# An attention and mixture-of-experts kernel: the first expert matrices are kept on the chip, and GpSimd's opening list has another order

## What is computed

```python
x = x + xattn(layernorm(x), ctx, mask, mask, Wq, Wkv, Wc)   # softmax(q k^T / sqrt(8)) v, then Wc
xf = layernorm(x).reshape(-1, 128)
top_vals, top_idx = top_k(xf @ router_w.T, 2)
probs = softmax(top_vals)
for e in range(8):
    w = sum(where(top_idx == e, probs, 0))
    h = gelu(xf @ w1[e].T + b1[e])         # 128 -> 512
    out = out + w * (h @ w2[e].T + b2[e])  # 512 -> 128
x = x + out
```

## Time and profile before

| | |
|---|---|
| median of three runs | 394.74 us |
| the profiled execution's own time | 396.63 us |
| its span, first to last instruction | 394.9 us |
| PE busy | 325.1 us (82%) |
| DVE, ACT, POOL busy | 253.1, 231.7, 231.8 us |
| chain that ended last, by engine | PE 65%, DVE 13%, issue 9%, ACT 6%, DMA 3%, POOL 1% |
| read from HBM | 34.90 MB |
| moved by DMA | 59.94 MB |

### The profile page before, as it was taken

One profiled execution on the slowest core, in us unless ns is written; L12 is line 12 of the kernel. 1 busy time (PEld: TensorE's weight loads), 2 busy tenths in 40 slices (PEclk: granted clock), 3 DMA queues, 4 the chain that ended last, 5 costly groups with the idle time before them and its releaser, 6 DMA issues.

```text
span 394.9 us, 11551 instructions
## 1 busy us (share of the span) xinstructions
PE 325.1 (82%) x3721; PEld 260.3 (66%) x3721; DVE 253.1 (64%) x751; ACT 231.7 (59%) x567; POOL 231.8 (59%) x384
## 2 busy tenths in 40 slices
PE   2659699999979898978787976969899999999950
PEld 1226466666656665656555865968789999999840
DVE  4855779999868778769943623645554555446762
ACT  2313569798868768667766423545456666566530
POOL 8745252724758567563667487565766656565550
PEclk9999989999999899999996888999999999999995
DMA  4664463555535424411143563666547767659946
GB/s 131 179 176 114 111 187 96 99 129 161 146 100 142 123 76 120 126 46 45 32 118 99 171 188 108 180 204 185 170 123 254 216 207 213 179 184 317 295 137 186
DMA packets 60618, 59.94 MB, mean 152 GB/s; under 512 B 13797, under 2 KB 45188, under 8 KB 60560
## 3 DMA queue, kind: packets, MB, share of 16 engines
q1 hardware_dynamic: 53504, 46.61, 42.6%
q0 software_dynamic: 4320, 8.47, 6.2%
q10 hardware_dynamic: 2736, 4.13, 3.3%
HBM read 34.90 MB, written 11.63 MB: 118 GB/s over the span
## 4 chain that ended last, share of the span: by engine, by line
PE 65%; DVE 13%; issue 9%; ACT 6%; DMA 3%; POOL 1%; another core or an unknown queue 1%; SPq 0%; DVEq 0%; POOLq 0%; ACTq 0%
PE sexp L1196 16%; PE smax L1184 16%; PE smax L1062 7%; PE tail L1106 7%; DVE shift L1351 4%; PE feed L1053 2%; PE feed L1038 2%; ACT probs L871 2%; PE prep L1130 2%; PE sexp L1070 2%; PE heads L1122 2%; PE feed L1048 2%; PE prep L1137 1%; DMA stacks<-result_d 1%
## 5 line engine op out<-in xcount | busy, mean ns | idle before, releaser
L1351 DVE TENSOR_REDUCE shift<-smax 128x4 f32<-128x512 f32 x128 | 87.0, 682 | 35.1 <-PE smax L1062 34.0
L1184 PE MATMUL smax<-probs,w_ring 128*128 128x128 f32 x568 | 79.2, 284 | 14.3 <-issue 12.8
L793 POOL DMA_INDIRECT result_d<-y_out,stacks x71 | 70.8, 997 | 30.5 <-issue 28.8
L1184 PEld LDWEIGHTS smax<-probs,w_ring 128*128 128x128 f32 x568 | 71.2, 197 | 17.7 <-issue 17.2
L871 ACT ACTIVATE probs<-sexp 128x512 f32<-128x512 f32 x128 | 74.4, 595 | 12.9 <-PE sexp L1070 11.6
L704 POOL DMA_INDIRECT dispatch_d<-rows_out,row_i x64 | 63.0, 984 | 30.6 <-issue 14.8
L1196 PE MATMUL sexp<-w_sb,probs 128*128 x568 | 78.6, 282 | 2.0 <-ACT probs L1005 1.2
L1826 DVE TENSOR_TENSOR probs<-smax,b_cols 128x512 f32<-128x512 f32 x71 | 49.0, 691 | 44.3 <-issue 15.9
L1196 PEld LDWEIGHTS sexp<-w_sb,probs 128*128 128x128 f32 x568 | 70.5, 195 | 5.8 <-issue 5.6
L1005 ACT ACTIVATE probs<-probs 128x512 f32<-128x512 f32 x71 | 44.8, 631 | 37.3 <-DVE probs L1826 27.3
L1062 PE MATMUL smax<-stacks 64*128 64x128 bf16 x512 | 51.3, 230 | 17.2 <-DVE shift L1351 9.7
(11 more groups left out here) (221 smaller groups left out, 502.6 us busy)
## 6 DMA issues: line engine op xcount, KB each, us to landing
w_ring<-w_t_dram SPq DMA_DIRECT2D x71, 256.0 KB
stacks<-kpart SPq DMA_DIRECT2D x46, 128.0 KB
stacks<-qpart SPq DMA_DIRECT2D x46, 128.0 KB
stacks<-dispatch_d SPq DMA_DIRECT2D x71, 65.0 KB
stacks<-result_d ACTq DMA_DIRECT2D x12, 256.0 KB
xw<-x_dram SPq DMA_DIRECT2D x8, 256.0 KB, 3.3
w_sb<-w_t_dram SPq DMA_DIRECT2D x8, 256.0 KB
out_dram<-xw SPq DMA_DIRECT2D x8, 256.0 KB
```

The costliest lines, as they stand in the source:

```text
L793: nc.gpsimd.indirect_dma_start(out=result_d, out_offset=bass.IndirectOffsetOnAxis(ap=xg[r][:, D + 1:D + 2].bitcast(U32), axis=0), in_=y_ou ...
L1184: last = nc.tensor.matmul(up_ps[i][:, c * P:(c + 1) * P], w1_ring[t % WRING][:, c * P:(c + 1) * P], xg_t[i], start=True, stop=True)
L1351: nc.vector.tensor_reduce(shift4[n % 2][:, hp, 0, 4 * m:4 * m + 4], smax[hp][:], AX.X, ALU.max, negate=True).then_inc(max_taken, 1)
```

## The change

A tile `w1_sb` of 128 partitions holds all eight w1 (16 KB a partition). SP loads one of them in each of the slots 2, 6, ..., 30, behind what else it does in the slot (`w1_here` counts them), and waits for all eight ahead of the first ring load. `load_w1` then copies the expert's part from `w1_sb` into the ring; ring, semaphores and order stay. In POOL's opening list `clear_queries(1)` and `set_keys(1)` change places around `split_low(0)`, `prepare_values(0)` goes ahead of the second row scales, and the third part of group 1's queries goes behind slot 0's `split_shift`.

```diff
--- before.py
+++ after.py
@@ -154,6 +154,7 @@
 
         router_sb = sb("router_sb", [P, EXPERTS])
         w1_ring = [sb(f"w1_ring{i}", [P, FF]) for i in range(WRING)]
+        w1_sb = sb("w1_sb", [P, EXPERTS, FF])
         w2_sb = sb("w2_sb", [P, EXPERTS, FC, D])
         b1_cols = sb("b1_cols", [P, EXPERTS * FC])
         b2_sb = sb("b2_sb", [P, EXPERTS * D])
@@ -327,6 +328,7 @@
         w2_loaded = sem("w2_loaded")
         xg_loaded = [sem(f"xg_loaded{i}") for i in range(TRING)]
         w1_loaded = [sem(f"w1_loaded{i}") for i in range(WRING)]
+        w1_here = sem("w1_here")
         xg_turned = sem("xg_turned")
         xg_copied = sem("xg_copied")
         up_done = sem("up_done")
@@ -493,6 +495,9 @@
                 if g is not None and g >= RING:
                     sp.wait_ge(v_done, g - RING + 1)
                     load_ctx(g)
+                if s % GB == 2:
+                    e = s // GB
+                    sp.dma_start(w1_sb[:, e:e + 1], w1_t[:, e:e + 1]).then_inc(w1_here, 16)
                 if s and s % GB == 0:
                     e = s // GB - 1
                     sp.dma_start(w2_sb[:, e:e + 1], w2_t[:, e:e + 1]).then_inc(w2_loaded, 16)
@@ -513,7 +518,7 @@
 
                 if t >= WRING:
                     sp.wait_ge(up_done, t - WRING + 1)
-                sp.dma_start(w1_ring[r][:], w1_t.rearrange("p e f -> p (e f)")[:, bass.ds(e * FF, FF)]).then_inc(w1_loaded[r], 16)
+                sp.dma_start(w1_ring[r][:], w1_sb[:].rearrange("p e f -> p (e f)")[:, bass.ds(e * FF, FF)]).then_inc(w1_loaded[r], 16)
 
             def store_pad(at):
                 sp.dma_start(dispatch_d[bass.ds(at, P), :], pad_row[:]).then_inc(pads_sent, 16)
@@ -521,6 +526,7 @@
             sp.wait_ge(table_steps, FIRST_STEPS)
             experts = table_values(mybir.EngineType.SP, expert_of, 0, EXPERTS - 1)
             starts = table_values(mybir.EngineType.SP, start_of, 0, EXPERTS * REGION)
+            sp.wait_ge(w1_here, 16 * EXPERTS)
             for t in range(AHEAD):
                 load_w1(t, t, experts[t])
             sp.wait_ge(sexp_done, UNITS * OLD_BATCHES)
@@ -635,15 +641,14 @@
             set_keys(0)
             clear_queries(0)
             query_scale(0)
+            clear_queries(1)
+            split_low(0, krest, kpart, k_split)
             set_keys(1)
-            split_low(0, krest, kpart, k_split)
-            clear_queries(1)
+            prepare_values(0)
             query_scale(1)
             scale_rows(1)
-            prepare_values(0)
             split_low(1, krest, kpart, k_split)
             query_scale(2)
-            split_low(1, qrest, qpart, q_split)
 
             def constants():
                 nc.gpsimd.iota(iota_i[:], [[1, EXPERTS]], base=EXPERTS, channel_multiplier=0).then_inc(iotas_made, 1)
@@ -724,6 +729,7 @@
                 if 0 < s <= BATCH:
                     split_shift(s - 1)
                 if s == 1:
+                    split_low(1, qrest, qpart, q_split)
                     set_keys(2)
                 if s == 2:
                     clear_queries(2)
```

## The result

The changed kernel took 401.85 us (median of 4 runs, 401.43 to 403.97) beside 394.93 us for the kernel before on the same chip (4 runs): a ratio of 1.0139, 95% interval 1.0091 to 1.0187. It is slower by 1.4%, and outside the range of the prediction. The profiled execution has a span of 399.8 us (before 394.9).

The account below looks back on a forecast made before the run. PE was taken to bound attention and the expert tiles, with engines waiting for each other in the opening. -0.75 and -2.1 us, with 0 for loads and loop, gave -2.85: 394.74 to 391.9 us, range 387.5 to 396.

Parts of the forecast that it names:

- The opening: GpSimd's reordered list up to the first scores: xq's gain is given back, qpart gains; -0.75 us, between 0.4 and -1.65.
- the turn: Behind the first scores, PE no longer waits for POOL's shift, so next scores start earlier; -2.1 us, bounds -1.5 and -2.44.
- slot 4's first maximum: Sign in attention of the profile after: slot 4 comes some 2.9 us earlier.
- The sum of -2.85 us for the order: GpSimd's new list: -0.75 us up to the first scores and -2.1 us behind them.
- Rival C: Opening: PE's speed rise stays where it is in time, half the gain comes back; -1.4 us, 393.3 us; chance 0.23.
- The eight loads and SP's wait at 0: Attention: eight 256 KB w1 loads on SP's queue and the wait for them cost 0, loads from 0 to +1 us.
- the loop stays PE's: 0: Expert tiles: copies from SBUF fit under PE's 1.91 us a tile, so the loop changes by 0.
- 1.16 + 0.48 us a tile: Tile loop's DMA engines: 1.16 us for the 256 KB copy, 0.48 for all else; 1.64 us, under 1.91.
- Rival D: Tile loop: copies out of SBUF become its bound; at 165 GB/s +9.6 us, 401.5 us in all; chance 0.13.
- Its second form: Tile loop: copies slow PE's own reads; 2.1% on 71 x 1.91 us would eat the whole gain; within the 0.13 chance.

Follow-up runs that it names:

- ring from DRAM: The changed kernel, with the eight resident loads and the wait, but the ring filled from DRAM as before; 0.9920 of before on chip B, 0.9965 on D.
- ring only: Against the kernel before: ring filled from the resident copy in SBUF, GpSimd's opening list in its old order; 1.0176 of before on chip B, 1.0226 on D.
- e9: Against the kernel without copies: whole copies from register-held SBUF addresses run beside PE, nothing reads or waits for them; 1.0088 of before on chip B.
- e4: The changed kernel without ring copies: PE reads the resident copy at a fixed expert, the expert's choice is left out; 0.9920 of before on chip B.

## Why the prediction was wrong

- **The opening: right, step by step.** Xq 0.69 us (0.69 said), moment_sum ended at 15.19 (15.2), qpart 0.70 (0.69), first scores at 20.31 (20.3), the turn at 26.28 (26.3), slot 4's first maximum 2.7 us earlier (2.9). The port held as the rows of before had shown it: what the COPY gave to xq it took from diff_sq. One detail differs: of the two small operations behind mean_diff only diff_sq stopped for the COPY; the ADD before it started with the COPY, at 11.50, and took 0.15 us.
- **The sum of -2.85 us for the order: right in size.** Alone the order gave -0.78% on B (3.1 us, 1.3 to 5.0) and -0.48% on D (1.9 us, 0.6 to 3.2). Rival C, in which the rise of PE's speed stays where it is in time and takes half of the gain back, falls: PE's score matmuls go from 0.31 to 0.22 us each at 39.93 us, before at 42.62, and attention stays some 3 us ahead.
- **The eight loads and SP's wait at 0: right** (0.9920 with, 0.9922 without).
- **The step that failed is "the loop stays PE's: 0".** It put the copies at nothing because their own time on the DMA engines, 1.16 + 0.48 us a tile, is under 1.91. That condition held, with room to spare: no DMA is among PE's waits, and in the changed kernel the engines' share is no higher than before:

```profile
300.00:340.00 40.00, 39.95 (x354) 39.56 (x353) 20.60 (x42) 26.23 (x62) 24.08 (x41) 1.00 0.61 200
```

  By that share a copy took some 0.7 us (an estimate, 0.61 x 1.91 - 0.48), not 1.16. What the sum has no term for is what a copy out of SBUF costs work that doesn't wait for it. Measured, that is 6.6 us on chip D, by the kernels that differ in the source of the ring alone. By the means of the stages, whole copies from a register-held place against none or DRAM, it is 3.7 us in tiles 2 to 30, 1.0 in tiles 30 to 63 (a tile costs 0.03 us more) and 1.0 in tiles 63 to 70, together 5.7. Only the last of these has a shown path, PE's register load at tile 64, which the prediction doesn't name. For tiles 2 to 30 the cause stays open: PE's idle time there (15.8 to 17.6 us in three profiles, 12.9 to 16.8 in six) and its time at half clock (some 9 to 18 and 7 to 11 us, estimated from the mean granted clock) overlap between the two sorts of kernel.
- **Rival D had the sign, with 0.13, and not the mechanism; that its 401.5 us lies beside the measured 401.85 is chance.** Copies too slow for the loop would have shown in PE's waits and as a longer tile throughout. Its second form, copies that slow PE's own reads, falls as well: on chip D the median of a first-product matmul is 275 ns in both kernels (ring from DRAM, then changed):

```profile
L1190 PE MATMUL smax<-probs,w_ring x568: 275/275/553, 213.6 to 376.9; 128*128 128x128 f32 x190
```

```profile
L1190 PE MATMUL smax<-probs,w_ring x568: 275/275/561, 213.2 to 381.3; 128*128 128x128 f32 x190
```

  The rule that the prediction cited from the Trainium skill, page "SBUF — State Buffer", section "SBUF: two separate sides", that a transfer doesn't slow an engine's access, agrees with these rows. The slowed accesses that the rows show are the sequencers' register loads. The Trainium skill's page "Runtime: NRT & Kernel Launch", section "Instruction fetch mechanics", says of register loads from HBM that each is a round trip over AXI. If those from SBUF go the same way, they belong to the transfers; the loads of 1.9 us (changed) and 2.8 us (ring only, both on chip D) fit that, and no run here shows the path itself.

What stays open: by what path the copies cost 3 to 4 us in tiles 2 to 30, why a register-held place in SBUF costs more than a fixed one (or the order in which the places are read does), how GpSimd's sends and PE's gaps hang together, and why chip C showed so little of the loss.

## What to carry to other kernels

A transfer that no one waits for isn't free (e9 lost 1.7% against e4), so look, besides bandwidth, at what the sequencers do beside it, register loads above all. A gap that is longer in one profile of after than in one of before may be there without the change as well: look for it in the kernel with half of the change. Moving a source nearer to save DRAM traffic is worth nothing where a DRAM ring already costs as much as no ring, and that one comparison, ring from DRAM against no copies, can be made first. Where runs spread and chips differ, set each half of a change beside the whole on one chip before a loss is explained.

## What the runs showed of the hardware

- Issuing a 256 KB copy of 128 rows took SP 333 ns from DRAM with a register-held address, 471 ns from SBUF at a fixed place, 492 ns from SBUF at a register-held one; the DRAM load issued behind it took 452 in place of 333 ns.
- A register load of up to eight values took PE 0.60 to 0.74 us at the median; the one at tile 64 took 1.07 to 1.08 us with the ring from DRAM or small copies, 1.5 to 2.8 us beside whole copies out of SBUF, and what it took more was added to the stage (0.84 and 0.85 us on chip D).
- The granted clock fell to 0.50 for some 3.4 us after PE had waited 1.85 us behind such a load (e9); after a wait of 2.25 us (ring only, chip D) it stayed at 1.00.
- A COPY of 128x2048 on GpSimd stopped a four-element DVE operation with two SBUF operands for 1.74 us, and a MEMSET a TENSOR_SCALAR for 1.76 us; a four-element ADD that started with the COPY took 0.15 us.
